# Graph layer on one core: the aggregation of four destination groups with source slices stationary, 500 destinations moving, and transposed sums that VectorE turns and device memory puts back in rows

## What is computed

```python
def _L0_gnn_ref(x, W, edge_w, src, dst):
    support = jnp.matmul(x, W)
    messages = support[src] * edge_w[:, None]
    out = jax.ops.segment_sum(messages, dst, num_segments=N_NODES)
    return out
...
xn = _layernorm(x, axis=-1)
x = x + _L0_gnn_ref(xn, L0_gnn_W, edge_weight, src, dst) + _L0_mix_ref(xn[None], ...)[0]
x = x + _L0_ffn_ref(_layernorm(x, axis=-1)[None], L0_ffn_w_gate, L0_ffn_w_up, L0_ffn_w_down)[0]
```

## Time and profile before

| | us |
|---|---|
| median of 3 runs | 1667.86 |
| the profiled execution, its own time | 1668.56 |
| its span, first to last instruction | 1666.6 |
| PE busy | 1643.1 |
| DVE busy | 1115.9 |
| ACT busy | 487.1 |
| aggregation, first to last matmul | about 986.5 to 1540 |

### The profile page before, as it was taken

The page is one execution under the profiler, slowest core; times in us unless marked ns, Lnnn a source line. Parts: engine busy times, 40 slices in busy tenths (PEclk is TensorE's granted clock), DMA queues, the critical chain, the costliest instruction groups (busy, mean ns, idle before and its releaser), DMA issues.

```text
span 1666.6 us, 22401 instructions
## 1 busy us (share of the span) xinstructions
PE 1643.1 (99%) x7896; PEld 1333.1 (80%) x7896; DVE 1115.9 (67%) x2568; ACT 487.1 (29%) x591; POOL 636.8 (38%) x497
## 2 busy tenths in 40 slices
PE   7999999999999999999999999999999999999998
PEld 6899999877777888887788878878777877777665
DVE  7866583576777766755555566676775674774885
ACT  4632311322111111123311023333333232332554
POOL 2011465777777777776688304410300000000000
PEclk9999999999999999999999999999999999999999
DMA  9999888765686755567866656555555345433554
GB/s 314 350 418 347 310 262 252 187 141 122 151 210 146 196 146 131 136 150 176 236 135 136 148 157 198 178 170 162 139 171 138 113 121 136 138 113 93 148 172 124
DMA packets 154777, 302.89 MB, mean 182 GB/s; under 512 B 61624, under 2 KB 92392, under 8 KB 154713
## 3 DMA queue, kind: packets, MB, share of 16 engines
q1 hardware_dynamic: 78469, 206.81, 39.5%
q0 software_dynamic: 66192, 62.07, 17.1%
q10 hardware_dynamic: 10052, 33.26, 6.6%
HBM read 202.88 MB, written 99.20 MB: 181 GB/s over the span
## 4 chain that ended last, share of the span: by engine, by line
PE 85%; DVE 7%; DMA 5%; SPq 1%; issue 1%; ACT 1%; DVEq 0%; ACTq 0%
PE PS L377 21%; PE PS L378 21%; PE PS L379 21%; PE PS L1543 5%; PE PS L1545 5%; PE PS L1544 5%; PE PS L1794 4%; DMA Aside<-A_dense 3%; PE PS L1824 2%; PE PS L1609 2%; DVE SL L1310 1%; DVE stats L1337 1%; DVE zr L1331 1%; DVE AL L1312 1%; DMA z<-zx 1%
## 5 line engine op out<-in xcount | busy, mean ns | idle before, releaser
L726 POOL DMA_INDIRECT A_dense<-wtot,cell x333 | 532.7, 1600 | 213.3 <-DMA A_dense<-wtot,cell 121.2
L377 PE MATMUL PS<-SL,AH 125*125 125x512 f32 x784 | 309.0, 394 | 3.5 <-DVE AL L1312 3.4
L378 PE MATMUL PS<-SH,AL 125*125 125x512 f32 x784 | 310.3, 396 | 0.0
L379 PE MATMUL PS<-SH,AH 125*125 125x512 f32 x784 | 310.1, 396 | 0.0
L377 PE MATMUL PS<-WL,xtH 128*125 128x512 f32 x640 | 251.9, 394 | 0.9 <-DVE xtL L1199 0.8
L378 PE MATMUL PS<-WH,xtL 128*125 128x512 f32 x640 | 251.5, 393 | 0.0
L379 PE MATMUL PS<-WH,xtH 128*125 128x512 f32 x640 | 251.3, 393 | 0.0
L1310 DVE TENSOR_TENSOR SL<-S,SH 125x1024 fp32r<-125x1024 f32 x98 | 119.6, 1221 | 137.6 <-ACT SH L954 137.6
L954 ACT ACTIVATE SH<-S 125x1024 fp32r<-125x1024 f32 (+1 forms) x98 | 104.1, 1062 | 346.1 <-PE PS L379 345.9
L377 PEld LDWEIGHTS PS<-SL,AH 125*125 125x125 f32 x784 | 145.8, 186 | 44.0 <-DVE AL L1312 6.8
L378 PEld LDWEIGHTS PS<-SH,AL 125*125 125x125 f32 x784 | 146.1, 186 | 36.3
(11 more groups left out here) (191 smaller groups left out, 2606.2 us busy)
## 6 DMA issues: line engine op xcount, KB each, us to landing
A_dense<-zeros POOLq DMA_DIRECT2D x40, 1280.0 KB
xt<-xnT SPq DMA_DIRECT2D x60, 500.0 KB
Araw<-A_dense SPq DMA_DIRECT2D x100, 250.0 KB, 2.7
Aside<-A_dense SPq DMA_DIRECT2D x100, 250.0 KB, 3.0
keyrow<-key_rows SPq DMA_DIRECT2D x42, 512.0 KB
ewrow<-weight_rows SPq DMA_DIRECT2D x42, 512.0 KB
xnT<-XT ACTq DMA_DIRECT2D x20, 500.0 KB, 8.2
zx<-in_x SPq DMA_DIRECT2D x20, 448.0 KB
```

Of the source, the lines that this page charges most:

```text
L377: nc.tensor.matmul(o, lh, rl, start=start, stop=False)
L378: nc.tensor.matmul(o, ll, rh, start=False, stop=False)
L379: return nc.tensor.matmul(o, lh, rh, start=False, stop=stop)
L726: pool.indirect_dma_start(cells[m], bass.IndirectOffsetOnAxis(cell[:, col:col + 1], 0), wtot[:, col:col + 1], None, compute_op=ALU.add).th ...
```

## The change

Groups 0 to 3 are aggregated the other way round. A slice of 128 features of `SH` or `SL` is stationary, and all 500 destinations of `AH` or `AL` move (`by_slice`); bank k then holds the sums of 128 features by 500 destinations, 8 banks x 3 = 24 matmuls for a source. Group 4 keeps the old form (`by_row`). What follows from that:
- **Turning.** In place of `add_z`, DVE turns the banks in blocks of 32 x 32 into `sums_in` (`turn_sums`, four instructions of 128 x 1024, two banks each). For the blocks to land right, `S` is stored with its features in another order (`sources_out`), and the last group's `add_z` reads its banks in that order.
- **Round trip.** ACT writes `sums_in` to device memory (`sum_d`) in 8 DMAs of 256 KB, in runs of 1 KB; POOL waits for them (`sums_back`) and loads them as rows into `sums_by_row`, 2 x 1 MB. At pairs 3 and 4 DVE adds them to `zr` (`add_rows`, 4 instructions of 125 x 1024, new).
- **Moved.** Statistics go to pairs 3 and 4, moments, deviation and the write of `r_d` to the end of pair 4, rounding to pairs 5 to 8, ACT's `integers` to pairs 6 to 9. The load of `zr` is split into four of 0.5 MB at pairs 6 to 9. Chunks 9, 10 and 11 go to pairs 1, 2 and 9 of group 1.
- Loops over pairs are written out on DVE and ACT.

The core of the diff:

```diff
@@ PE
+        def by_slice(i, sh, sl, d, first, last_one):
+            for k in range(2 * d, 2 * d + 2):
+                cols = slice(k * P, (k + 1) * P)
+                last = product3(PS[:, k, 0:GN], sh[:, cols], sl[:, cols], AH[i][0:ROWS, :], AL[i][0:ROWS, :], first, last_one)
+            return last
...
-                rows = slice(d * ROWS, (d + 1) * ROWS)
-                for c in range(2):
-                    cols = slice(c * 512, (c + 1) * 512)
-                    last = product3(PS[0:ROWS, 2 * d + c, :], AH[i][0:ROWS, rows], AL[i][0:ROWS, rows],
-                                    sh[:, cols], sl[:, cols], first, last_one)
+                if by_row:
...
+                else:
+                    last = by_slice(i, sh, sl, d, first, last_one)
@@ DVE
+        def turn_sums(g):
+            for d in ORDER:
+                wait_banks(g, d)
+                nc.vector.transpose(sums_in[:, :, 64 * d:64 * d + 64].rearrange("p c (b i) -> p b c i", b=2),
+                                    PS[:, 2 * d:2 * d + 2, :].rearrange("p b (c j) -> p b c j", j=32)).then_inc(s_r[d], 1)
+
+        def add_rows(g, tiles):
+            dve.wait_ge(s_zin, g * (32 * GT) + 32 * GT)
+            dve.wait_ge(s_back, g * 64 + 64)
+            for d in tiles:
+                nc.vector.tensor_tensor(zr[0:ROWS, d, :], zr[0:ROWS, d, :], sums_by_row[0:ROWS, d, :],
+                                        ALU.add).then_inc(s_res, 1)
...
+        def group(g, chunks=False, at_end=False):
+            for h in range(HALF):
+                m = g * HALF + h
+                low_of_sources(2 * h, 0, m)
+                sum_of_blocks(1, m)
+                if h == 0:
+                    turn_sums(g - 1)
+                if h in (ADD_PAIR, ADD_PAIR + 1):
+                    add_rows(g - 1, ((0, 1), (2, 3))[h - ADD_PAIR])
+                if h == QUANT_PAIR:
+                    inverse_deviation(g - 1)
+                d = h - QUANT_PAIR
+                if 0 <= d < GT:
+                    largest_r(g - 1, d)
+                if chunks and (g, h) in CHUNK_OF:
+                    round_chunk(CHUNK_OF[g, h])
+                low_of_sources(2 * h + 1, 1, m)
+                if not at_end or h + 1 < HALF:
+                    sum_of_blocks(0, m + 1)
+                if h in (ADD_PAIR, ADD_PAIR + 1):
+                    row_stats(g - 1, ((0, 1), (2, 3))[h - ADD_PAIR])
+                if h == ADD_PAIR + 1:
+                    row_moments(g - 1)
+                if 0 <= d < GT:
+                    round_r(g - 1, d)
+                if chunks and (g, h) in CHUNK_OF:
+                    turn_chunk(CHUNK_OF[g, h])
@@ ACT
             for d in range(GT):
                 act.wait_ge(s_r[d], g)
-            split_rows(act, r_d[move_rows(g - 1), :].rearrange("(t r) d -> r t d", r=ROWS), zr[:, :, :], s_rout)
...
+            for n in range(2):
+                for a in range(4):
+                    rows = sum_d[bass.ds(g - 1, 1), n * 256:(n + 1) * 256, a * 256:(a + 1) * 256]
+                    act.dma_start(rows.rearrange("o (c j) f -> (o j) c f", j=32),
+                                  sums_in[a * 32:(a + 1) * 32, n * 8:(n + 1) * 8, :]).then_inc(s_half[n], 16)
...
+                if h == ADD_PAIR + 1:
+                    deviation(g - 1)
+                    act.wait_ge(s_res, 32 + g * GT)
+                    split_rows(act, r_d[move_rows(g - 1), :].rearrange("(t r) d -> r t d", r=ROWS), zr[:, :, :], s_rout)
+
+        def load_z(g, d):
             act.wait_ge(s_rout, g * 32)
-            act.wait_ge(s_c5, g * GT)
-            split_rows(act, zr[:, :, :], z_d[move_rows(g), :].rearrange("(t r) d -> r t d", r=ROWS), s_zin)
+            act.wait_ge(s_c5, g * GT - GT + d + 1)
+            split_rows(act, zr[:, d, :], z_d[bass.ds(g * GN + d * ROWS, ROWS), :], s_zin)
@@ POOL
+        def sums_back(g):
+            for n in range(2):
+                pool.wait_ge(s_half[n], 32 + 64 * g + 64)
+                split_rows(pool, sums_by_row[:, 2 * n:2 * n + 2, :],
+                           sum_d[g, 2 * n * ROWS:2 * (n + 1) * ROWS, :].rearrange("(t r) d -> r t d", r=ROWS), s_back)
```

More of the change, by code:

```diff
@@ L239, in layer_kernel @@
     first_S = ((SH0, SL0), (SH1, SL1))
-    e3w = zone("E3w", cursor["E3"] + 12 * 2 * D, cursor["E3"] + TILES * 2 * D)
+    e3w = zone("E3w", cursor["E3"] + 4 * 2 * D, cursor["E3"] + 12 * 2 * D)
+    turned_at = cursor["E3"] + 12 * 2 * D
+    sums_in = zone("E3t", turned_at, turned_at + 16 * D)("sums_in", [P, 16, D // 4])
+    sums_by_row = zone("E3r", turned_at, turned_at + 16 * D)("sums_by_row", [P, GT, D])
     gwb = e3w("gwb", [P, 2, D])
@@ L277, in layer_kernel @@
     s_Azero = sems("s_Azero", 2)
-    s_acc = sems("s_acc", GT)
+    s_acc = {d: sem(f"s_acc{d}") for d in (0, 2, 3)}
     s_bd = sem("s_bd")
@@ L762, in _, with move_chunk @@
             load_chunk(c)
-        for c in range(12):
+        def move_chunk(c):
             if c + 2 < 12:
@@ L978, in high_beside_chunk @@
         def high_beside_chunk(g, h):
-            high_of_pair(g, h)
+            high_of_sources(h * 2, 0, g * HALF + h)
+            d = h - QUANT_PAIR - 1
+            if g and d >= 0:
+                integers(g - 1, d)
+            high_of_sources(h * 2 + 1, 1, g * HALF + h)
+            if g and d >= 0:
+                load_z(g, d)
             if (g, h) in CHUNK_OF:
@@ L991, in move_rows, with high_of_group @@
             return bass.ds(g * GN, GN)
[L993 to L996, removed]
+        def high_of_group(g, unrolled=False):
+            for i in range(2):
+                high_of_sources(i, i, g * HALF)
             for d in range(GT):
                 act.wait_ge(s_r[d], g)
-            split_rows(act, r_d[move_rows(g - 1), :].rearrange("(t r) d -> r t d", r=ROWS), zr[:, :, :], s_rout)
-            for h in range(2, 3 + GT):
+            for n in range(2):
[3 more added lines that the diff above has]
+                                  sums_in[a * 32:(a + 1) * 32, n * 8:(n + 1) * 8, :]).then_inc(s_half[n], 16)
+            for h in range(1, HALF):
+                if unrolled and (g, h) in CHUNK_OF:
+                    high_beside_chunk(g, h)
+                    continue
+                if not unrolled and h == 1:
+                    for i in range(2):
+                        act.wait_ge(s_fout[i], 128 * 6)
@@ L1426, in _ @@
[L1426 to L1431, removed]
+            low_of_sources(2 * h, 0, h)
+            sum_of_blocks(1, h)
+            round_chunk(CHUNK_OF[0, h])
+            low_of_sources(2 * h + 1, 1, h)
+            sum_of_blocks(0, h + 1)
+            turn_chunk(CHUNK_OF[0, h])
+        def group(g, chunks=False, at_end=False):
[25 more added lines that the diff above has]
+                    turn_chunk(CHUNK_OF[g, h])
@@ L1432, in _ @@
+        group(1, chunks=True)
         with dve.Fori(2, GROUPS - 1) as g:
             group(g)
[L1434 to L1439, removed]
+        group(GROUPS - 1, at_end=True)
         def scales_back(tiles):
@@ L1710, in _, with sources @@
         pe.wait_ge(s_fc, 3)
-        def sources(g, i, m, first, last_one, ends=False):
+        def by_slice(i, sh, sl, d, first, last_one):
[3 more added lines that the diff above has]
+            return last
+        def sources(g, i, m, first, last_one, ends=False, by_row=False):
             pe.wait_ge(s_lo5[i], m + 1)
@@ L1718, in sources @@
                     pe.wait_ge(s_r[d], g)
-                rows = slice(d * ROWS, (d + 1) * ROWS)
-                for c in range(2):
-                    cols = slice(c * 512, (c + 1) * 512)
-                    last = product3(PS[0:ROWS, 2 * d + c, :], AH[i][0:ROWS, rows], AL[i][0:ROWS, rows],
-                                    sh[:, cols], sl[:, cols], first, last_one)
+                if by_row:
+                    rows = slice(d * ROWS, (d + 1) * ROWS)
+                    for c in range(2):
+                        cols = slice(c * 512, (c + 1) * 512)
+                        last = product3(PS[0:ROWS, 2 * d + c, :], AH[i][0:ROWS, rows], AL[i][0:ROWS, rows],
+                                        sh[:, cols], sl[:, cols], first, last_one)
+                else:
+                    last = by_slice(i, sh, sl, d, first, last_one)
                 if last_one and d != ORDER[-1]:
@@ L1761, in first_sources @@
             for d in tiles:
[L1762 to L1766, removed]
+                last = by_slice(i, sh, sl, d, i == 0, False)
             return last
```

103 lines of the change are left out of this document (43 added, 60 removed).

## The result

The changed kernel takes 1682.88 us (median of four runs, 1679.57 to 1683.5), the kernel before 1667.59 (four runs). The ratio is 1.008, with a 95% interval of 1.0067 to 1.0094: slower by 0.8%, where 1659.8 and a gain were forecast. The time lies outside the range, and beyond rival B too, whose mechanism did not occur.

What follows compares the result with a forecast made beforehand. PE was taken to bound the kernel, the stage being as long as its matmuls are apart. Terms -10.2 + 2.0 + 0.6 - 0.5 = -8.1 gave 1659.8 us by the median, range 1655.4 to 1667.5.

Steps and rivals of the forecast that it cites:

- rival B: Group boundary: a turn out of PSUM takes 2.48 us, PE loses 4.4 us a group, 1677 us; chance 0.08.
- The eight stores on ACT: Group boundary: eight issues take 2.8 to 3.6 us, SH up to 1.2 us late with 2.5 spare; no cost.
- The burst that they start: Behind each boundary: stores compete with loads of Araw and Aside, 0.5 us a group, so +2.0 us.
- rival A: Pairs 1 and 2: store bursts and loads back cost 6 to 8 us, so 1664 to 1666; chance 0.17.
- Fewer columns: PE's matmuls in groups 0 to 3: 500 moving columns instead of 512, 9.8 to 10.9 us less, taken as -10.2.
- Turning, 1.24 us each: DVE at the boundary: four turns take 4.96 us in place of 4.52 for the additions; no cost.
- The way back: POOL's loads back: sums return by about +26 us, DVE needs them at about +31, 5 us spare; no cost.
- rival D: Sums come back 4 us late, DVE stands in add_rows with low parts queued behind: 14 us, 1674; chance 0.05.
- DVE's load: DVE over a group: busy time goes from 72 to about 77 of 109 us; no cost.
- Deviation at pair 4: End of pair 4: ACT free 2.3 us late against 2.5 spare, plus a table load in group 1; +0.6 us.
- zr by quarters: Load of zr in 0.5 MB bursts: removes PE's waits at pair 7 or so, -0.5 us.

Runs made afterwards that it cites:

- pool_stores: The changed kernel with the eight stores issued by POOL instead of ACT, POOL waiting for all eight before its first load back: 1659.37 us, ratio 0.9934.
- half_bytes: The changed kernel with eight ACT stores of 128 KB instead of 256 KB, no loads back, half the sums left out: 1653.48 us, ratio 0.9919.
- spread: The changed kernel with ACT issuing the same eight stores two at a time, behind four successive sources' high parts: 1658.44 us, ratio 0.994.
- no_trip: The changed kernel without the stores to device memory and the loads back, turned blocks added to zr straight from sums_in: 1655.63 us, ratio 0.9922.
- slices_alone: The kernel before with only the new matmul form in groups 0 to 3, sums added unturned in the old place: 1663.06 us, ratio 0.9957.
- stores_only: The changed kernel without the loads back; ACT's eight stores stay, DVE waits for them and adds sums_in: 1671.89 us, ratio 1.0018.

## Why the prediction was wrong

- **"The eight stores on ACT": the step that failed.** "2.8 to 3.6 us ... up to 1.2 us late ... Nothing." The place, the 2.5 us of spare time and what depends on it were right; the term was mis-sized. I took the price of an issue from a pair and from four stores of 128 KB, half the size, and multiplied by eight. Measured: 7.6 us, `SH` 4.9 us late. 4.9 - 2.5 gives 2.4 us a boundary; PE lost 2.5 to 2.8. `pool_stores`, `half_bytes` and `spread` each take the length of the issues off ACT, and with it the loss.
- **The trace of before had the price.** I looked only where ACT issues. SP's timeline in an early stage has six loads of 512 KB in a row; and the issue of `Aside` behind the write of r is itself long:

```profile
76.11 7.17 SPq L508 DMA_DIRECT2D raw<-in_L_mix_Wq  x6
...
1218.97 1.83 SPq L606 DMA_DIRECT2D Aside<-A_dense  x1
```

  That is 1.20 us for an issue, at twice the size of a store, and 1.83. Eight at 1.2 would be 9.6 us, over the 5.0 that were to be had (2.5 until `SH` is due and 2.5 spare): a loss at every boundary. It needed the question what an issue costs while much is already under way.
- **"The burst that they start", +2.0:** too small for the changed kernel, where the loads back alone cost 11 us, more than rival A had for the whole (6 to 8). The traffic alone doesn't do it: with ACT undisturbed (`pool_stores`), stores and loads back together add 3.7 us to `no_trip`, not to be told from the 2.0 or from nothing. (Rival A's "burst of only 7.5" is in no row: 2 MB at 321 GB/s are 6.4 us.) In the changed kernel the late `SH` moves the next `Aside` (1103.28) between the loads back, issued at 1100.04 and 1103.67, and it takes 12.75 us: the two terms were not independent.
- **Clock:** no term. About 5 us, in three stretches behind waits of 5.6, 2.8 and 2.8 us.
- **Fewer columns, -10.2:** right, if a little small: 11.6 by `SH`. But a gain in spacing is not a gain in time: `slices_alone` gives 7 of it.
- **Turning, 1.24 us each:** 1.215; rival B does not occur. The Trainium skill ("VectorE: DVE Perf Modes", section on the three transpose paths) has 311 ns for a square of 128 x 128 in bf16, which by estimate makes 2.49 us for eight; the row says half (1239 ns out of SBUF), and these runs say the same out of PSUM (1215).
- **The way back, no cost:** right, `add_rows` never waits; rival D does not occur. **DVE's load,** 77 of 109 us: DVE is busy 76.55 in groups of 112.8 to 115.6.
- **Deviation at pair 4, +0.6; zr by quarters, -0.5:** in `no_trip` all waits but the first make 0.6 us (before: 1.6), so the two terms, +0.1 together, came out at -1.0: neither the late deviation nor the write of r costs PE much.
- **The sum against the runs:** against the 1667.59 of the kernel before, -12.0 us without the way through memory and +3.7 for its traffic: -8.2, where -8.1 was forecast (by the ratio of `pool_stores`, -11.0). That they meet is in part luck, as the terms were off by a microsecond or two each. What the issues add on ACT, with the loads back that they shift, is the 23.5 us between 1659.4 and 1682.9.

A rule speaks to this. The Trainium skill ("DMA: Bandwidth & Descriptors", section "Issuing engines are not separate DMA queues") says that issuing from several engines saves only the time the sequencer needs to initiate a transfer, usually small beside the transfer. The first half agrees with the runs, as the bytes are no sooner through from POOL (13.1 us from the first issue to the release of the last load back; 11.4 from ACT, 1092.29 to 1103.67). The second misleads here: that time was 7.6 us, not small beside those 11.4, on an engine with 5 us of room, and taking it off that engine gave 23.5 of the 27 us back.

## What to carry to other kernels

Price an issue from the longest row of issues that the trace has, with their size beside it, not from one or two in an idle queue; then compare it with the room of the engine that issues, and of those that wait for that engine. Where the room is less, issue in twos between the engine's other work, or from an engine that nobody waits for. And make two sums for a stage that gets faster: the work that falls away, and the waits that this work used to cover.

## What the runs showed of the hardware

- Issues on ACT's queue grow with a backlog: of eight of 256 KB the fourth takes 1.25 us and the fifth 1.66; of four of 512 KB the third 1.95 and the fourth 2.23; of eight of 128 KB none over 0.52. In the kernel before, 2 MB are handed over by the write of r in two issues of 0.35 us, and the slow one is SP's, 1.8 us behind the first. So it is not the issuer's own queue alone. Here and at the eight stores the first slow issue comes 1.5 to 1.8 us behind the first of the burst. In `pool_stores`, where ACT issues none, one of SP's issues (`Aside`, at 1099.18) still takes 1.59 us, 5.6 us behind POOL's first store. Which limit is reached was not found.
- Eight issues on POOL take 4.63 us, 0.58 to 0.60 each, close to its eight issues of small stores just before (4.35). Whether they too would grow with more bytes was not tried.
- Runs of 1 KB or 8 KB make no difference to the issues (7.60 and 7.57 us).
- After a stop PE often ran at 1.2 GHz for some microseconds: at once behind the 5.6 us (the window at 0.51 above, some 7 us in all), and behind waits of 2.8 us after one to two microseconds at full clock, then for 3.4 us. Not always: two of the four waits of 2.5 to 2.8 us at the changed kernel's boundaries have none behind them. And the waits can be shorter: the first one of 1.7 to 1.8 us has such a stretch behind it in the kernel before, in `slices_alone` and in `stores_only`, and none in the changed kernel or in `no_trip`. A matmul is then 0.42 us behind the last in place of 0.23, about 1.5 us lost in 3.4.
